# Attention, post-norm and a routed block on one core: the block of eight groups fed from the attention's own transposed output, and a planner with other costs

## The reference

```python
qkv = x @ w_attn + b_attn                      # 256 -> 768
attn = softmax(q @ k.T / sqrt(256) + causal)   # 4096 x 4096 per batch
x1 = layernorm(x + (attn @ v) @ w_proj + b_proj)
scores = x1 @ w_router                         # top 3072 of 4096 rows per batch
out = x1, with gelu(x1 @ w_block) in the chosen rows
result = layernorm(x1 + out)
```

## Time and profile before

| | |
|---|---|
| Runs | 967.23, 967.45, 970.24 us (median 967.45) |
| Profiled execution | 969.85 us, span 968.1 us |
| TensorE, its weight loads | 940.7 us (97%), 806.6 us (83%) |
| VectorE | 769.6 us (79%) |
| ScalarE | 635.2 us (66%) |
| GpSimd | 274.3 us (28%) |
| DMA | 149.53 MB, mean 154 GB/s |
| Mean granted TensorE clock | 0.988 of full |

### The profile page before, as it was taken

One profiled execution on the slowest core, in us unless ns is written; L12 is line 12 of the kernel. 1 busy time (PEld: TensorE's weight loads), 2 busy tenths in 40 slices (PEclk: granted clock), 3 DMA queues, 4 the chain that ended last, 5 costly groups with the idle time before them and its releaser, 6 DMA issues.

```text
span 968.1 us, 15640 instructions
## 1 busy us (share of the span) xinstructions
PE 940.7 (97%) x5078; PEld 806.6 (83%) x5078; DVE 769.6 (79%) x1473; ACT 635.2 (66%) x993; POOL 274.3 (28%) x436
## 2 busy tenths in 40 slices
PE   9999999999999999999999999999999999998992
PEld 7889988888888888888888988888888888887771
DVE  4688996967966785789779989887899778568877
ACT  3566675764864585478555875686688558447985
POOL 3523124253042034513214253323203302111162
PEclk9999999999999999999999999999999999999996
DMA  6535344444253344567432533435777534336934
GB/s 190 175 123 171 110 142 121 121 130 141 76 164 104 104 151 158 165 213 228 153 126 82 186 111 108 164 94 180 241 237 251 172 100 131 119 100 219 314 131 174
DMA packets 85282, 149.53 MB, mean 154 GB/s; under 512 B 7761, under 2 KB 17618, under 8 KB 85202
## 3 DMA queue, kind: packets, MB, share of 16 engines
q1 hardware_dynamic: 85202, 148.54, 48.5%
HBM read 108.66 MB, written 39.85 MB: 153 GB/s over the span
## 4 chain that ended last, share of the span: by engine, by line
PE 93%; DVE 4%; issue 1%; ACT 1%; POOL 0%; ACTq 0%; DVEq 0%; POOLq 0%
PE sbank L514 37%; PE fbank L514 13%; PE obank L1048 11%; PE obank L1050 11%; PE obank L1049 11%; PE obank L1042 2%; PE obank L1044 2%; PE obank L1043 2%; PE fbank L1339 1%; PE fbank L1138 1%; PE mbank L946 1%; PE mbank L969 1%; DVE cmp L1502 1%; PE obank L554 1%; DVE tail L1751 0%
## 5 line engine op out<-in xcount | busy, mean ns | idle before, releaser
L514 PE MATMUL sbank<-qT,xT 128*128 128x512 f32 (+2 forms) x1728 | 413.2, 379 | 0.0
L514 PEld LDWEIGHTS sbank<-qT,xT 128*128 128x128 f32 x1728 | 306.4, 189 | 53.0 <-issue 0.3
L871 ACT COPY ring<-sbank 128x512 f32<-128x512 f32 (+3 forms) x288 | 157.5, 549 | 176.7 <-PE sbank L514 125.3
L1000 DVE TENSOR_TENSOR ring_lo<-ring,parts 128x1024 fp32r<-128x1024 f32 (+4 forms) x176 | 181.6, 1039 | 33.2 <-ACT parts L995 32.4
L1048 PE MATMUL obank<-ring_lo,vs 128*128 128x512 f32 x480 | 184.1, 384 | 4.1 <-ACT ot_sb L1107 1.6
L1050 PE MATMUL obank<-parts,vs 128*128 128x512 f32 x480 | 182.6, 380 | 0.0
L1049 PE MATMUL obank<-parts,vs 128*128 128x512 f32 x480 | 182.3, 380 | 0.0
L995 ACT CAST parts<-ring 128x1024 fp32r<-128x1024 f32 (+4 forms) x176 | 145.9, 834 | 52.4 <-PE obank L1050 39.7
L981 DVE TENSOR_TENSOR ring<-ring,mbank 128x1024 f32<-128x1024 f32 (+4 forms) x176 | 159.4, 946 | 9.4 <-PE mbank L969 9.4
L988 ACT ACTIVATE ring<-ring 128x1024 f32<-128x1024 f32 (+4 forms) x176 | 143.9, 845 | 24.7 <-DVE ring L981 24.4
L913 DVE TENSOR_TENSOR runmax<-ring,runmax 128x1024 f32<-128x1024 f32 x84 | 106.2, 1264 | 64.7 <-ACT ring L871 64.0
(11 more groups left out here) (222 smaller groups left out, 1204.7 us busy)
## 6 DMA issues: line engine op xcount, KB each, us to landing
vs<-v_scratch SPq DMA_DIRECT2D x288, 256.0 KB, 2.8
v_scratch<-vnew SPq DMA_DIRECT2D x30, 512.0 KB, 3.3
xres<-x SPq DMA_DIRECT2D x16, 512.0 KB, 4.7
out<-tail SPq DMA_DIRECT2D x32, 256.0 KB, 3.0
x_scratch<-xres SPq DMA_DIRECT2D x14, 512.0 KB, 3.1
y_scratch<-yb SPq DMA_DIRECT2D x14, 512.0 KB, 4.6
tail<-x_scratch SPq DMA_DIRECT2D x28, 256.0 KB, 3.5
tail<-y_scratch SPq DMA_DIRECT2D x28, 256.0 KB, 4.3
```

Source lines behind the costliest of these rows:

```text
L514: mm = eng.matmul(o, lhs(lh, k), rhs(rh, k), start=n == 0, stop=n == len(todo) - 1)
L871: act.copy(slot(n)[:, c0:], sbank[n % NSS][:, c0:]).then_inc(a_copy, 1)
L1000: dve.tensor_tensor(slots_lo(ns, c0), slots(ns, c0), f32(hi_of(u)), ALU.subtract).then_inc(v_lo, 1)
```

## The change

**The block in transposed form.** Groups that are turned and come before group 14 are now called `upright`: 3 to 7 and 11 to 13, eight of them. The block multiplies rows of x1, and those need channels on partitions. `ot_sb` has the attention's output that way already, undivided and before the residual. The new code completes it in place: SP stores the row of softmax sums (`sums_store`) and loads it back onto all partitions (`sums_load`), loads x transposed in two halves through one buffer (`rows_load`), VectorE makes (x + bias) * sums (`rows_scale`), GpSimd adds it to `ot_sb` (`rows_add`). The two buffers are halves of `yb`, so they wait until the y of the group before is stored. What is then in `ot_sb` is x + attention output, times the sum. The division by the sum and by the deviation is a scale of each row and is done in the Gelu's instruction (`up_gelu`, with `fscale` made by GpSimd), four of 256 columns in place of two of 512. The subtraction of the mean is moved into the weights: w_block loses the mean of each of its columns (`block_sums` on TensorE, two f32 matmuls, and one more product on VectorE in `block_parts`). The bias in channel form is made through DRAM at the start (`bias_store`, `bias_load`). `pe_t` and its two fills per group are gone for these eight; the 24 block matmuls stay, with other operands.

**Gelu held back.** `FAVOUR_US` gives single operations another weight and a later time in the planner: the softmax of group 15's first four units is preferred, and the Gelu of groups 5 and 13 is rated 20 us lower and counted ready 8 us later.

**Other costs.** DMA_US 1.6 to 2.0, GpSimd's fixed time 0.25 to 0.35, a narrow float32r matmul at least 0.11 in place of 0.06, and power by element.

```diff
+FAVOUR_US = {"last softmax z": (20, 0), "last softmax exp": (40, 0), "last softmax hi": (50, 0), "last softmax lo": (30, 0),
+             "last gelu": (-20, 8), "last block": (0, 0)}
-DMA_US, DMA_BYTES_US, FIRST_BYTES_US = 1.6, 320e3, 250e3
+DMA_US, DMA_BYTES_US, FIRST_BYTES_US = 2.0, 320e3, 250e3
-         "pool": (.25, 1 / 457, .1), "sp": (.45, 0.0, 0.0)}
+         "pool": (.35, 1 / 460, .1), "sp": (.45, 0.0, 0.0)}
-        self.time += max(.22 if passes == 4 else .06, ...)
+        least = .22 if passes == 4 else .11 if rhs.dtype == F32R else .06
...
+    upright = lambda G: not straight(G) and G < LATE
...
+            def block_sums(pe):
+                pe.wait_ge(ld_ffw, 32)
+                pe.wait_ge(g_const, 2)
+                for k in range(CC):
+                    mm = pe.matmul(w_sums, ones[:, :], wb[:, k, :], start=k == 0, stop=k == CC - 1)
+                mm.then_inc(p_wsum, 1)
...
+            def sums_load(sp):
+                sp.wait_ge(st_s, 16 * (nth + 1))
+                sp.wait_ge(st_y, 16 * G)
+                sp.dma_start(sums_wide, s_dram[G:G + 1, :].broadcast_to([P, GQ])).then_inc(ld_s, 16)
+
+            def rows_load(sp, c):
+                sp.wait_ge(st_y, 16 * G)
+                if c:
+                    sp.wait_ge(g_rt, CC * nth + c)
+                sp.dma_start(rows_wide, xt_rows[b][:, c, g * GQ:(g + 1) * GQ]).then_inc(ld_xr, 16)
+
+            def rows_scale(dve, c):
+                dve.wait_ge(ld_xr, 16 * (CC * nth + c + 1))
+                dve.wait_ge(ld_s, 16 * (nth + 1))
+                dve.scalar_tensor_tensor(out=rows_wide, in0=rows_wide, scalar=b_cols[:, c:c + 1], in1=sums_wide, op0=ALU.add,
+                                         op1=ALU.mult).then_inc(v_sx, 1)
+
+            def rows_add(pool, c):
+                pool.wait_ge(v_sx, CC * nth + c + 1)
+                filled(pool, ("o", G, 1))
+                pool.tensor_tensor(ot_sb[:, c, :], ot_sb[:, c, :], rows_wide, ALU.add).then_inc(g_rt, 1)
+
+            def up_fhi(act, j):
+                act.wait_ge(g_rt, CC * (nth + 1))
+                act.copy(up_hi(j), ot_sb[:, :, 2 * j * P:2 * (j + 1) * P]).then_inc(a_fhi, 1)
...
+            def up_block(pe, j):
+                pe.wait_ge(v_flo, 2 * G + j + 1)
+                freed(pe, ("ff", G, j))
+                for t in range(2):
+                    mm = split3(pe, bank_of(("ff", G, j))[:, t * C:(t + 1) * C],
+                                lambda h, k: (up_lo if h else up_hi)(j)[:, k, t * P:(t + 1) * P],
+                                lambda h, k: WB[:, h, k, :], CC)
+                mm.then_inc(p_out, 1)
+
+            def up_gelu(act):
+                act.wait_ge(g_fs, nth + 1)
+                for j in range(2):
+                    filled(act, ("ff", G, j))
+                    for t in range(2):
+                        op = act.activation(y_pair(G, j)[:, t], bank_of(("ff", G, j))[:, t * C:(t + 1) * C],
+                                            ACT.Gelu_apprx_tanh, scale=fscale[:, G % 2, 2 * j + t:2 * j + t + 1])
+                    op.then_inc(a_gelu, 1)
```

More of the change, by code:

```diff
@@ L126, in tensor_tensor @@
         if op == ALU.pow:
[L127 removed]
+            self.time += .2 * int(np.prod(out.shape[1:]))
         return self.two(out, in0, in1)
@@ L639, in prepare @@
             pe_fill["values weights"] = [lambda pe, m=m, k=k: values_weights(pe, m, k) for m in range(CC) for k in range(CC)]
-            pe_fill["values weights"] += [lambda pe, m=m: query_sums(pe, m) for m in range(CC)] + [bias_product, bias]
+            pe_fill["values weights"] += [lambda pe, m=m: query_sums(pe, m) for m in range(CC)] + [bias_product, bias, block_sums]
             def a_parts(dve):
@@ L977, in softmax @@
             G, ns, c0 = units[u]
+            first = G == len(groups) - 1 and u < first_unit[G] + QT
             def z(dve):
@@ L983, in z @@
                                   ALU.subtract).then_inc(v_z, 1)
-            at("dve", "softmax z", z)
+            at("dve", "softmax z", z, "last softmax z" if first else None)
             def exp(act):
@@ L988, in exp @@
                 act.activation(slots(ns, c0), slots(ns, c0), ACT.Exp, scale=SCALE).then_inc(a_exp, 1)
-            at("act", "softmax exp", exp)
+            at("act", "softmax exp", exp, "last softmax exp" if first else None)
             def hi(act):
@@ L995, in hi @@
                 act.copy(hi_of(u), slots(ns, c0)).then_inc(a_hi, 1)
-            at("act", "softmax hi", hi)
+            at("act", "softmax hi", hi, "last softmax hi" if first else None)
             def lo(dve):
@@ L1000, in lo @@
                 dve.tensor_tensor(slots_lo(ns, c0), slots(ns, c0), f32(hi_of(u)), ALU.subtract).then_inc(v_lo, 1)
-            at("dve", "softmax lo", lo)
+            at("dve", "softmax lo", lo, "last softmax lo" if first else None)
         last_values = []
@@ L1802, in program @@
                 for make in pe_fill[f] if isinstance(pe_fill[f], list) else [pe_fill[f]]:
-                    at("pe", name, make)
-        queue, times = merged(streams)
+                    at("pe", name, make, "last block" if f[0] in ("ft", "ff") and f[1] == LATE - 1 else None)
+        queue, times = merged(streams, favours)
         srch[0] = pool_steps[0] = 0
```

96 lines of the change are left out of this document (80 added, 16 removed).

## The result

| | before | after |
|---|---|---|
| Median | 968.91 us (966.92 to 971.57, 10 runs) | 964.69 us (962.21 to 967.43, 10 runs) |
| Profiled execution | 969.85 us, span 968.1 | 965.09 us, span 963.3 |

The ratio is 0.9954, with a 95% interval of 0.9938 to 0.9971: 4.2 us faster by the medians, 4.8 by the profiled executions. The forecast was 962.3 from a median of 967.45 (5.1 less), the range 958.5 to 967.5. For the profiled execution the prediction's sum gave 964.7 us; it took 965.09.

What follows compares the result with a forecast made beforehand. TensorE's work was taken to bound the kernel up to 877 us. Transposes 7.0 less block_sums 0.5 less the later spreading 1.4 gave 5.1 us off the 967.45 median: 962.3 us, range 958.5 to 967.5.

Steps and rivals of the forecast that it cites:

- The transposes: TensorE in eight groups: 16 blocks of four transposes go, 0.44 us each, 7.0 us less, all on the path.
- block_sums: Two added f32 matmuls of 128x256 on TensorE, 0.24 us each: 0.5 us more on the path.
- The new chain: Additions, load, product, cast and difference ahead of each new block: 10.0 us, fitting everywhere, 3.9 us to spare in group 13.
- Rival C: Slower: the new chain comes late by hand-overs 1.3 us late each, 8.6 us in all; 971.0 us, chance 0.11.
- the allowance for SP's queue: V loads behind the store of y and next xT: taken as 0, up to 1 us in each of eight places.
- VectorE's added work: Two products of 128x512 per group, 0.745 us each, 12 us in all; priced at nothing as throughput.
- Body waits: TensorE's waits before group 15, for the running maximum and qT: 2.2 us, expected worth nothing either way.
- Rival A: Better planner costs also remove the body's 2.2 us of waits and some of the clock's 1.6; 959.5 us, chance 0.22.
- The spreading behind the dozen: Start of group 15: 12 block matmuls now stand ahead of mcol, so TensorE idles 1.44 us more.
- The clock: Lower clock behind the wait for parts in group 15 cost 1.6 us before; change -1.6 to +2, taken as 0.
- from there to the end the distances are unchanged: From the last group's mcol, 5.1 us earlier, to the end of the kernel: no distance changes.
- rival B: Start of group 15: longer low clock, up to 2 us, and late value loads eat most gain; 965.5 us, chance 0.18.

Runs made afterwards that it cites:

- experiment 1: Changed kernel with four identity transposes put back ahead of each of the 16 new blocks, order untouched; 969.87 us, ratio 1.0023 to the kernel before.
- experiments 5: Changed kernel with the two f32 matmuls of block_sums issued twice, the planner not told; 964.98 us.
- experiment 9: Changed kernel with only VectorE's queue altered: the last group's four router-weight products (L1339) put behind the next three ring_lo; 961.61 us, ratio 0.9917.
- Experiments 2: Kernel before with the planner's new costs alone; 972.41 us, ratio 1.0044.
- Experiments 2 and 3: The second of these: changed kernel with the planner's old costs, new block and held Gelu kept; 968.48 us, ratio 0.9992 to the kernel before.
- experiments 4: Changed kernel planned so that the last group's spreading of maxima stands ahead of the second dozen of group 13's block matmuls; 962.26 us, ratio 0.9929.
- experiment 10: Changed kernel with the last spreading ahead of group 13's second dozen block matmuls and L1339 behind the next three ring_lo; 959.84 us, ratio 0.9899.

## Why the prediction was right, and where its terms were off

**The transposes.** 7.0 us predicted; experiment 1 has 6.4 to 6.7. Right, and read rightly: from start to start, not from the record's duration.

**block_sums.** 0.5 us predicted, 0.8 to 1.2 measured (experiments 5 and 9 and the profile after). The mis-sized term: I divided a busy time by a count of records as if each were a matmul. The 6.4 to 6.7 us that went, less these 1.2, are also the 5.3 us by which TensorE's busy time fell; I had said 6.5.

**The new chain** beside it was priced at nothing, and no wait for v_flo, the new block's input, is in the profile after. Rival C is out; the allowance for SP's queue (0, up to 8 us) was 0 too: of the waits in the body none is a DMA's. Pricing VectorE's added work at nothing was right for the time, but its size was wrong, 23 us for 12. The 16 new products take 13.0 us (812 ns each where I took 745). The rest is old work that takes longer: the products with the router's weights went from 455 to 517 ns on average (L1260, now L1320), the causal mask from 306 to 374 (L879, now L929). That fits two engines holding each other up, as the last section shows for other rows; for these it is not shown.

**Body waits.** Taken as unchanged at 2.2 us; they fell to 1.0. Rival A had a piece of the truth. Experiments 2 and 3 show that this is luck of the order: with the costs alone or the block alone they grew, to 2.8 and 4.8.

**The spreading behind the dozen.** 1.44 us predicted, 1.43 measured by experiments 4 and 10 from runmax to mcol, with the wait for ot_sb at 3.3 us (I had said 3) and the parts 10.8 us behind mcol, as before.

Together: -6.7 + 1.2 - 1.2 + 1.4 = -5.3 us at mcol; the profile has -5.9. The 0.6 us between are not attributed.

**The clock.** Taken at 0 net, and it was 0, but not as the old trace had it: the low stretch moved from 887 to 900 us.

**Behind the parts.** The step "from there to the end the distances are unchanged" failed. The distance grew by 1.4 us at 900.52, since VectorE stood in front of ring_lo with work that was due 25 us later. The trace of before had this wait at 0.89 us without a releaser, and I did not ask what VectorE did ahead of it. In kind this was rival B, a late arrival in group 15. B's 965.5 lies nearer to the median of 964.7 than 962.3 does, and its gain of 1.9 us lies further from the 4.2 measured than the forecast's 5.1. B blamed value loads and the clock, and neither was the cause. The sum came out 0.9 us too good (4.2 for 5.1). That it is so near is in part luck: the unforeseen 1.4 us and the 0.7 of block_sums were mostly paid by the body's waits (1.2), by the 0.6 us that are not attributed and, in the profiled execution, by a tail that is 0.6 us shorter.

## What to carry to other kernels

When the list of waits gives no releaser, set the start of the waiting instruction against the ends on every other engine before blaming the DMA: here a VectorE operation ended 0.1 us before it. In a planned queue, work that is due late but becomes ready early belongs behind the operations that the bounding engine is about to need. And when a scheduler redraws the order, time the parts of a change together: apart they measured +4 and 0, together -4.2.

## What the runs showed of the hardware

**VectorE and GpSimd slow each other.** L1339 takes 1.51 us when it starts beside GpSimd's L1152 and 0.42 to 0.43 otherwise. In experiment 9 two ring_lo overlap L1152 (start, us):

```profile
893.65 2.33 DVE L1051 TENSOR_TENSOR ring_lo<-ring,parts 128x1024 fp32r<-128x1024 f32 x1
896.04 2.18 DVE L1051 TENSOR_TENSOR ring_lo<-ring,parts 128x1024 fp32r<-128x1024 f32 x1
```

and GpSimd between them:

```profile
894.86 2.28 POOL L1152 TENSOR_TENSOR xres<-xres,b_tot 128x512 f32<-128x512 f32 x1
```

2.33 and 2.18 us in place of 1.22, and 2.28 in place of the 1.36 that is the median of L1152. The ends follow each other as if the two took turns: VectorE at 895.98, GpSimd 1.16 us later at 897.14, VectorE 1.08 us later at 898.22. The Trainium skill ("SBUF — State Buffer", SBUF: two separate sides) says that the two engines share a pair of ports as an exclusive lock, which a VectorE instruction with two inputs in SBUF, against a GpSimd instruction that reads SBUF, or that GpSimd instruction holds to its end, whichever starts first. The trace agrees: the excess of 1.0 to 1.1 us is no more than one L1152.

**A low stretch at the start, in some profiles.** The granted clock in 16 to 20 us, in the changed kernel and in experiment 9, whose programs are the same there:

```profile
16.00:20.00 4.00, 4.00 (x11) 3.00 (x11) 1.99 (x3) 2.09 (x2) 2.51 (x2) 0.59 0.75 273
```

and

```profile
16.00:20.00 4.00, 4.00 (x25) 3.67 (x24) 3.08 (x3) 3.01 (x4) 2.75 (x2) 1.00 0.73 256
```

The profiles of before, of the changed kernel and of experiment 10 have 0.57 to 0.59 there, those of the others 1.00. The last pause of TensorE ahead of that stretch ended at 8.8 to 8.9 us in the three and at 7.9 to 8.5 in the others. The second mcol of the changed kernel stands at 61.01 us, 2.4 us later than its twin in experiment 9 (58.61): 0.75 us of these by the later end of that pause (8.89 for 8.14), 1.65 by the clock. Two profiles are compared rightly only when both have that stretch or neither: before and after both do. How many of the timed executions without a profile have it is not known, so it may be part of any difference of 2 us between two medians here.

**The same idle time does not always bring the clock down.** Waits for ot_sb of 3.25 and 3.26 us were followed by a clock of 1.00 in the changed kernel and by the lower level in experiment 9 (0.50 in 872 to 876 us), waits of 1.84 and 1.83 us by the lower level in experiment 4 and by 1.00 in experiment 10. Whether experiment 10 (no low stretch up to 908 us) owes part of its lead to that:

```profile
872.00:908.00 36.00, 32.90 (x154) 27.28 (x155) 35.13 (x49) 33.59 (x45) 6.32 (x4) 1.00 0.95 317
```

is left open; its five runs lie within 1.3 us of each other.
